# Routing half of the batches beside the first stage, and the other half beside the first expert tiles

## What is computed

```python
emb = word_emb[input_ids] + pos_emb
g_j = relu(mean_g(adj_j @ word_emb[ids_j]) @ W_j.T + b_j)      # three graphs
h = layernorm(concat([emb, broadcast(g_1, g_2, g_3)]) @ W_proj.T + b_proj) * gamma + beta
u = layernorm(h)
h = h + causal_conv(u, k) + u * bias                           # k: 128 taps per channel
x = layernorm(h)
top2, idx = top_k(x @ Wr.T, 2);  w = softmax(top2)
h = h + sum_k w[k] * (gelu(x @ Wi[idx[k]].T + bi) @ Wo[idx[k]].T + bo)
```

## Time and profile before

| | us |
|---|---|
| median of three runs (989.84 to 992.35) | 991.18 |
| span of the profiled execution | 995.9 |
| first stage, to the end of the last projection | 349.5 |
| convolution, to its last matmul | 413.3 |
| routing and first fetch, to the first up matmul | 502.4 |
| 71 tiles, to the last down matmul | 979.5 |
| last scatters | 996.0 |

### The profile page before, as it was taken

How to read it: one execution, slowest core, us unless ns; L and a number is a source line. 1 busy time by engine, 2 the same in 40 slices (tenths; PEclk the granted TensorE clock), 3 DMA queues, 4 the chain that set the end, 5 groups by cost and what they waited for, 6 DMA issues and landing times.

```text
span 995.9 us, 22850 instructions
## 1 busy us (share of the span) xinstructions
PE 869.3 (87%) x7469; PEld 822.9 (83%) x7469; DVE 656.0 (66%) x2142; ACT 536.0 (54%) x1271; POOL 644.7 (65%) x552
## 2 busy tenths in 40 slices
PE   3959898998898739893889999999999999999993
PEld 2959898998898738892679999999999989898993
DVE  3167857776867565978756776666667656666662
ACT  1222223213312325599667777777777767677761
POOL 6777777777777300100067886777778768788886
PEclk9957556556756669996699999999999999999997
DMA  8437547457465429855946446745744543343454
GB/s 245 131 87 248 179 153 257 136 200 225 157 207 195 126 86 282 225 166 131 245 101 149 61 60 158 191 61 122 199 83 63 130 96 61 59 60 59 61 57 44
DMA packets 99788, 138.31 MB, mean 139 GB/s; under 512 B 13427, under 2 KB 81430, under 8 KB 97654
## 3 DMA queue, kind: packets, MB, share of 16 engines
q0 software_dynamic: 39552, 53.26, 28.1%
q1 hardware_dynamic: 59142, 73.59, 24.3%
q10 hardware_dynamic: 1008, 10.34, 2.8%
HBM read 98.14 MB, written 39.02 MB: 138 GB/s over the span
## 4 chain that ended last, share of the span: by engine, by line
PE 29%; DMA 22%; POOL 22%; issue 12%; DVE 8%; ACT 4%; DVEq 2%; SPq 1%; POOLq 0%; ACTq 0%
DMA out<-Hs,id_s 20%; POOL ev_g L521 13%; POOL emb_g L512 5%; PE bank L799 3%; PE bank L801 3%; PE bank L800 3%; POOL blob L537 3%; PE bank L780 2%; PE bank L781 2%; PE bank L784 2%; PE bank L783 2%; PE bank L782 2%; DVE hstats L1157 2%; ACT adj_s L956 1%; PE bank L763 1%
## 5 line engine op out<-in xcount | busy, mean ns | idle before, releaser
L975 ACT ACTIVATE Hs<-bank,U 128x256 bf16<-128x256 f32 x426 | 214.0, 502 | 126.0 <-PE bank L784 126.0
L551 POOL DMA_INDIRECT out<-Hs,id_s x142 | 233.5, 1645 | 65.6 <-issue 45.6
L537 POOL DMA_INDIRECT blob<-xtab_d,id_g x142 | 151.6, 1068 | 122.7 <-DVEq L1340 79.6
L521 POOL DMA_INDIRECT ev_g<-in_word_emb,ids_i x192 | 189.7, 988 | 58.5 <-issue 57.9
L976 ACT ACTIVATE Hs<-bank,U 128x256 f32<-128x256 f32 x426 | 216.4, 508 | 0.0
L799 PE MATMUL bank<-U,Hs 128*128 128x192 bf16 x852 | 210.0, 246 | 0.3 <-issue 0.3
L801 PE MATMUL bank<-U,Hs 128*128 128x192 bf16 x852 | 208.8, 245 | 0.0
L800 PE MATMUL bank<-U,Hs 128*128 128x192 bf16 x852 | 208.5, 245 | 0.0
L1362 DVE TENSOR_TENSOR Hs<-Hs 128x512 bf16<-128x512 f32 x213 | 146.8, 691 | 92.1 <-ACT Hs L976 92.0
L780 PE MATMUL bank<-wst,U 128*128 128x256 bf16 x426 | 116.6, 274 | 1.3 <-DVE wst L1351 1.3
L781 PE MATMUL bank<-wst,U 128*128 128x256 bf16 x426 | 116.7, 274 | 0.0
(11 more groups left out here) (216 smaller groups left out, 1643.2 us busy)
## 6 DMA issues: line engine op xcount, KB each, us to landing
adj_s<-in_adj SPq DMA_DIRECT2D x48, 256.0 KB, 7.3
ev_g<-kpad_d SPq DMA_DIRECT2D x24, 512.0 KB, 5.8
U<-blob_d SPq DMA_DIRECT2D x14, 771.0 KB, 5.0
wst<-in_wsrc SPq DMA_DIRECT2D x8, 1344.0 KB
blob_d<-blob ACTq DMA_DIRECT2D x7, 1443.0 KB
U<-blob_d SPq DMA_DIRECT2D x14, 672.0 KB, 5.7
xtab_d<-U SPq DMA_DIRECT2D x4, 1552.0 KB, 17.0
out<-Hs SPq DMA_DIRECT2D x4, 1536.0 KB, 12.8
```

The source lines that it names most:

```text
L521: pool.indirect_dma_start(ev_g[:, p, j, b, :], None, t["word_emb"], bass.IndirectOffsetOnAxis(ap=ids_i[:, 1 + j, i * Q + b:i * Q + b + 1], ...
L537: pool.indirect_dma_start(xg_f[:, q % RX, h, :], None, xtab_d, bass.IndirectOffsetOnAxis(ap=id_g[:, 2 * q + h:2 * q + h + 1], axis=0)).the ...
L551: pool.indirect_dma_start(out, bass.IndirectOffsetOnAxis(ap=id_s[:, 2 * q + h:2 * q + h + 1], axis=0), yo[:, q % RY, h, :], None, compute_ ...
L975: f(hh[w][:, d, :], ps, ACT.Gelu, bias=bi[:, d:d + 1])
```

## The change

The batches are cut into two halves of 32. The convolution, the scores, the ranks and the sorting are written as a generator `route(x)` for each engine, which does one small step per call, and `advance(route, n)` does n steps.

- `route(0)`, for batches 0 to 31, is interleaved with groups 8 to 15 of the first stage; the tables `beside` say how many steps stand before and behind the group's projection (on ACT: at its end).
- Of the first half's choices, only full tiles are taken, the first `TA = 25` of them; what is left over goes with the second half's. The number of tiles stays 71.
- `route(1)`, for batches 32 to 63, is interleaved with tiles 1 to 24 by `pieces(q)`. Before tile 25 all engines finish it and start the fetches anew.
- A matmul of the convolution still moves 128 columns (now four channels' worth of 32, of which one is wanted), so that each half takes 192 of them.
- `W3` goes from 3 to 2, `RY` (rooms for results) from 4 to 3. The PSUM banks are dealt out anew: the graph results share bank 0 with the column means, so `graph_vectors(i)` waits for the copy of the means of group i + 1; `project` has one pair of banks.
- The splitting of expert weights goes on one expert per group (0 to 7), with two rooms; SP issues all stores of them. The Toeplitz loads of the first half are issued by ACT, those of the second by SP between the weight reloads.
- Loops on registers are written out.

```diff
@@ constants @@
-RING = 4
+RING = 5
-W3 = 3
+TA = 25
+W3 = 2
+WK = 3
-RY = 4
+RY = 3
...
@@ sync @@
+            for q in range(WB, NT):
+                while given < min(UNITS, 4 * q - 1):
+                    next_toep(given)
+                    given += 1
+                if q == 10:
+                    store_rows(1)
+                if q == TA - 1:
+                    store_inputs(1)
+                if q == TA:
+                    sp.wait_ge(eid_done, 2)
+                reload_up(q, q % WB)
+                if q > WB:
+                    reload_down(q - 1, (q - 1) % WB)
...
@@ tensor @@
             def graph_vectors(i, p):
-                pe.wait_ge(cs_ready, i + 1)
+                pe.wait_ge(cs_ready, min(i + 2, NQ))
...
+            def route(x):
+                pe.wait_ge(rows_done, NA * (x + 1))
+                if x:
+                    pe.wait_ge(eid_done, 1)
+                at_conv = conv_bank[x]
+                for u in range(UNITS):
+                    c = u // 2
+                    pe.wait_ge(turned[x], u + 1)
+                    if u % 2 == 0:
+                        after(pe, conv_read[x], c - len(at_conv) + 1)
+                    place = bank[at_conv[c % len(at_conv)]]
+                    for k in range(CC):
+                        at = u % 2 * CC + k
+                        n = min(128 // HALF, 2 * CC - at)
+                        last = mm(place[:, at * HALF:(at + n) * HALF], tp[x][u % 2][:, k, :],
+                                  Ut[x][:, u * CC + k:u * CC + k + n, :].rearrange("p c b -> p (c b)"), start=True, stop=True)
+                    last.then_inc(conv[x], 1)
+                    yield
...
+                pe.wait_ge(conv_read[x], CHUNKS)
+                turn_pair(0)
+                yield
+                for h in range(PAIRS):
+                    if x == 0 and h + 1 < PAIRS:
+                        turn_pair(h + 1)
+                    score(h)
+                    if x == 1 and h + 1 < PAIRS:
+                        turn_pair(h + 1)
+                    yield
...
+                for g in range(TG):
+                    pe.wait_ge(hot_p_ready[x], g + 1)
+                    pe.wait_ge(hot_s_ready[x], g + 1)
...
+            early = route(0)
+            beside = {8: (0, 4), 9: (2, 4), 10: (2, 4), 11: (2, 4), 12: (2, 9), 13: (0, 8), 14: (1, 9), 15: (0, 8)}
...
+                graph_features(i)
...
+                advance(early, beside.get(i, (0, 0))[0])
+                project(i, p)
...
+                advance(early, beside.get(i, (0, 0))[1])
...
+            def pieces(q):
+                if 1 <= q <= 6:
+                    return 2, 0, 2
+                if 7 <= q <= 11:
+                    return 1, 1, 1
+                if q == 12:
+                    return 1, 0, 1
+                if q in (14, 15):
+                    return 1, 0, 0
+                return (1, 0, 1) if 16 <= q < TA - 1 else (0, 0, 0)
...
+                up_tile(q)
+                if q + 1 < NT and q + 1 != TA:
+                    turn_rows(q + 1)
+                advance(late_route, n[0])
+                if q > 0:
+                    down_half(q - 1, 0)
+                    advance(late_route, n[1])
+                    down_half(q - 1, 1)
+                advance(late_route, n[2])
+                if q + 1 == TA:
+                    for _ in late_route:
+                        pass
+                    turn_rows(TA)
@@ scalar @@
+                if x == 0:
+                    act.wait_ge(kpad_stored, 32)
+                    act.wait_ge(w_lo, E - 1)
+                    for u in range(RING):
+                        load_toep(act, x, u)
+                    act.wait_ge(w_out[0], 16 * E // 2)
...
+                for g in range(TG):
+                    scaled(g)
+                    for b in range(2 * g, 2 * g + 2):
+                        row_part(b)
+                    yield
+            beside = {8: 6, 9: 6, 10: 6, 11: 6, 12: 8, 13: 9, 14: 9, 15: 8}
...
@@ vector: the steps of route(x): 12 additions, statistics, variances, choices and sum,
@@ scales, slots, shares, 16 pairs of one-hots, ids @@
+            beside = {8: (0, 2), 9: (1, 2), 10: (1, 2), 11: (1, 2), 12: (1, 2), 13: (0, 2), 14: (1, 9), 15: (0, 8)}
...
+                if 1 <= i <= E:
+                    split_lo(i - 1)
+                if i + 2 < NQ:
+                    row_sums(i + 2, p)
+                advance(early, beside.get(i, (0, 0))[0])
+                rows(i, p)
...
+                advance(early, beside.get(i, (0, 0))[1])
...
+            def pieces(q):
+                if q == 1:
+                    return 0, 1
+                if 2 <= q <= 6:
+                    return 1, 1
+                if q == 7:
+                    return 1, 1
+                if q == 8:
+                    return 1, 0
+                if q == 13:
+                    return 1, 1
+                if q == 14:
+                    return 0, 1
+                if q == 15:
+                    return 1, 1
+                return (1, 1) if 16 <= q < TA - 1 else (0, 0)
...
                 split_hidden(q, q % W3, (0, 2))
-                if 0 < q < NT - 1:
+                advance(late_route, n[0])
+                if 0 < q < NT - 1 and q + 1 != TA:
                     transposed(q + 1, (q + 1) % W3)
                 split_hidden(q, q % W3, (4,)).then_inc(hid, 1)
                 if q > 0:
                     bias_out(q - 1)
+                advance(late_route, n[1])
```

More of the change, by code:

```diff
@@ L86, in after @@
                 eng.wait_ge(semaphore, value)
[L88 to L95, removed]
         out_rows = out[0:B * S, :].rearrange("(b s) d -> b s d", s=S)
@@ L657, in _ @@
-            column_means(0, 0)
-            steps(pe, NQ // 2, pair, last=1)
-            pe.wait_ge(rows_done, NQ)
-            def chunk(it, s):
-                c = it * RING + s
-                pe.wait_ge(turned, c + 1)
-                for k in range(CC):
-                    n = 2 if k < CC - 1 else 1
-                    last = mm(bank[6 + s % 2][:, k * B:(k + n) * B], tp[:, s % 2, k, :],
-                              Ut[:, bass.ds(c * CC + k, n), :].rearrange("p c b -> p (c b)"), start=True, stop=True)
-                last.then_inc(conv, 1)
@@ L696, in score @@
-            def score(i):
-                p = i % 2
-                g = next(k for k, (first, n) in enumerate(GROUPS) if i * Q < first + n)
-                pe.wait_ge(xnT_ready, i + 1)
-                after(pe, chosen, g - 1)
-                for h in range(Q // 2):
-                    at_h = (i * Q - GROUPS[g][0] + 2 * h) * E
-                    for r in range(XR):
-                        last = mm(bank[3 + g % 2][:, at_h:at_h + 128], xnT[:, p, XR * h + r, :], wr[:, r, :], start=r == 0, stop=r == XR - 1)
-                last.then_inc(logits, 1)
@@ L883, in _ @@
-            column_copy(0, 0)
-            steps(act, NQ // 2, pairs, last=1)
-            def turn(it, s):
-                act.wait_ge(toep_in[s], 16 * (it + 1))
-                after(act, conv, it * RING + s - 1)
-                f(tp[:, s % 2, :, :], reverse(toep[:, s, :, :]), ACT.Copy).then_inc(turned, 1)
-            turn(0, 0)
-            turn(0, 1)
-            normal(NQ - 1, 1)
-            for s in range(2, RING):
-                turn(0, s)
-            with act.Fori(1, NCH // RING) as it:
-                for s in range(RING):
-                    turn(it, s)
@@ L948, in _ @@
[L948 to L957 removed]
+                p = e % 2
+                act.wait_ge(w_in[p], 48 * (e // 2 + 1))
@@ new lines, in _ @@
+            early = route(0)
+            beside = {8: 6, 9: 6, 10: 6, 11: 6, 12: 8, 13: 9, 14: 9, 15: 8}
+            column_copy(0, 0)
+            for i in range(NQ):
+                p = i % 2
+                embedding_copy(i, p)
+                if i < NQ - 1:
+                    column_copy(i + 1, 1 - p)
+                graphs(i, p)
+                if i == 0:
+                    filter_decay()
+                    filter_sine(1)
+                if i > 0:
+                    normal(i - 1, 1 - p)
+                if i < E:
+                    split_hi(i)
+                advance(early, beside.get(i, 0))
@@ L959, in row_hi @@
+            normal(NQ - 1, 1)
+            for _ in early:
+                pass
+            f(junk[:, :], mean_w[:, 0:1], ACT.Gelu)
             def row_hi(q):
@@ L1394, in _ @@
                     bias_out(q - 1)
+                advance(late_route, n[1])
+                if q + 1 == TA:
+                    for _ in late_route:
+                        pass
+                    row_lo(TA)
+                    transposed(TA, TA % W3)
             bias_out(NT - 1)
```

1079 lines of the change are left out of this document (544 added, 535 removed).

## The result

| | before | after | forecast |
|---|---|---|---|
| median, us | 991.8 | 1185.3 (1182.2 to 1186.8) | 1074 |
| ratio of the times | 1 | 1.1937 [1.188, 1.1994] | 1.083 |
| span of the profiled execution | 995.9 | 1182.2 | 1078.9 |
| first up matmul, F | 502.4 | 552.2 | 472.4 |
| what the second half adds, X | | 136.5 | 113 |

The change makes the kernel 19% slower. The direction was right, the size was not: 193 us more where 83 were forecast, and the time lies far above the range. By the sum of the prediction, X = 1182.2 - 995.9 - (552.2 - 502.4) = 136.5. So of the 103 us that the forecast's span is short, 80 are in F and 23.5 in X. F didn't fall by 30 us, it rose by 50.

The account below looks back on a forecast made before the run. Gathers were taken to pace the first stage, with TensorE 90% busy, and TensorE the tiles. Span 995.9 us, less 30 for an earlier first up matmul, plus 113 from the second half, times 0.9953: 1074 us, range 1050 to 1095.

Parts of the forecast that it names:

- Groups 0 to 7: First stage: the added wait for the next column means' copy costs 1 us (bounds 0 and 6.4); VectorE's weight split is hidden.
- Groups 8 to 12: First stage beside the first half's convolution: 27.2 us per group in 9 to 12, plus 5 us for late Toeplitz loads.
- Group 14: First stage: one-hots queue behind VectorE's rows, TensorE idles about 17.5 us; group 13's projection to group 15's takes 78 us.
- From group 15 to the tiles: After group 15's projection, in series: rows 13.9, picks 11.4, table store 8, fetch to first up matmul 6.9; 40 us.
- Tiles 1 to 6: Second half's convolution beside these tiles: 24 units of 1.8 us add 43 us to TensorE, plus 2 for waits.
- Tiles 7 to 12: Second half's turn and score: 16 pairs at 1.25 us add 20 us, plus 2 for the wait on the last addition.
- Tiles 13 to 15: VectorE's choices, scales and slot step delay copies that TensorE needs; 2 x 2.1 us caught up, 14 us added.
- Tiles 16 to 23: Two picks per tile give ACT 8.7 us of work against 6.6 per tile, adding 17 us.
- The last tiles: Tile stage: output ring of three instead of four costs 0; additional expert weight reloads cost 4 us (0 to 20).
- the rival with the full clock: Full clock holds in groups 8 to 13, waits by order stay: 1034 us; chance 0.23.
- the one paced by the gathers: Gathers still pace the first stage, TensorE's free time takes the first half's work: 962 us; chance 0.06.
- The rival with late transfers: Toeplitz loads, weight reloads and refill at their upper bounds add 30 us: 1104 us; chance 0.14.

Follow-up runs that it names:

- The load order: Kernel after, with SyncE issuing the load of expert i before the store of expert i-1: 1149.2 us, ratio 1.1555.
- the new bank: Kernel after, with graph results of groups 0 to 7 in PSUM bank 3, so graph_vectors waits only for its own group's column copy: 1144.9 us, ratio 1.1511.
- three repairs: Kernel after, with expert loads ahead of stores, a separate bank for early graph results, and picks ahead of projection in groups 14 and 15: 1110.8 us, ratio 1.1182.
- The picks' repair: Kernel after, with one-hots ahead of rows in groups 14 and 15 and group 15's picks ahead of its projection: 1160.1 us, ratio 1.1664.

## Why the prediction was wrong, and where it was right

- **Groups 0 to 7: the step that failed.** "Bounds 0 and 6.4; I take 1" priced the added wait by the 0.17 us copy and its 0.8 us delay, as if the copy came as early as before. I asked who is queued behind the wait on TensorE, but not what is queued ahead of the copy on ScalarE, and ahead of that on SyncE. The next sentence, that the split is "hidden", went by VectorE's busy share and left out the store and the load around it. The step cost 57 us where 1 was taken. The load order, the new bank and both together (with the picks) gave 36, 40 and 75 us, and group 8 back at 204.9.
- **Groups 8 to 12** lost 13 us more than forecast. The sum per group was close: 27.7, 29.4 and 31.0 us measured, 27.2 forecast; from the end of group 8's projection to that of group 9's it took 38.4 where 32.2 were due. I gave the first five Toeplitz loads 5 us, bounds 0 and 10, as a matter of bandwidth. What the trace shows is that ScalarE stands while it issues them, 9.9 us; moving them gave F 2.8.
- **Group 13**: 27.6 us forecast, 33.9 measured. Two terms were too small. A step of turn and score, 11 records in my count, takes 1.5 us and not 1.25; and at a granted clock of 0.55 from the graph vectors on, the rest of the group took some 21 us for 17.2.
- **Group 14** was right in mechanism and size: 17.5 us idle forecast, 17.0 measured, and from group 13's projection to the one of 15 78 us forecast, 79 measured. That the picks can be had earlier by their order alone was shown too; the ids, left behind `rows(15)`, kept some 12 us of that from F.
- **From group 15 to the tiles**: 44 us for the 40 forecast. Norm, picks and store took 13.5, 11.4 and 7.9 for 13.9, 11.4 and 8. The fetch took 10.6 (541.68 to 552.23) for 6.9, with four weight loads and several Toeplitz loads issued beside it. That the weight loads slow it isn't borne out: with the picks first they are issued 8 to 12 us ahead of the fetch, and it still took 9.6 (523.80 to 533.39). The cause stays open.
- **Tiles 1 to 6**: 45 forecast, 44.1 measured, TensorE full: right. Only the floor of 11 us right below was not seen.
- **Tiles 7 to 12**: 22 forecast, 29.5 measured. It is the same step of turn and score: 16 of 1.5 us (672.71 to 674.22 in tile 9) are 24 for my 20, and TensorE waits 3.6 us for my 2, all at tile 7, where the clock falls as well.
- **Tiles 13 to 15**: 14 forecast, 20.9 measured. The mechanism was right, VectorE's copies queued behind the choices and slots. TensorE's two waits for them are 15.7 us; I had let 2 x 2.1 us be caught up by VectorE's slack. No experiment separates these terms.
- **Tiles 16 to 23**: 17 forecast, 23.4 measured. ScalarE is the pacer, as forecast; the sum of 8.7 us of its work per tile left no gap, and the tile took 9.15.
- **Tile 25**: 11 forecast, 13.1 measured. **The last tiles**: "the same here: 0" for the ring and 4 for the weight reloads. From tile 26 to tile 70 the kernel after takes 10 us more than before, and its tail 5 less. Luck helps here: the sum is close to my 4, but the 10 us vary from trace to trace, and no run parts the ring from the reloads.
- **The rivals.** TensorE's clock in groups 8 to 13 stayed as forecast, partly lost in every group, so the rival with the full clock falls, and so does the one paced by the gathers. The rival with late transfers had the right kind of cause, but not the place.
- **The whole.** With three repairs F is 479 and the time 1111: 37 us above the forecast. Of this 22 are X and 6.6 F. The rest is the factor between span and median, which I took as 0.9953 and which came out above 1: in every run the time is about 1.8 us more than the span of the same execution, while the profiled span of before, 995.9 us, is longer than that kernel's median time. That F comes so close is luck in part. The picks' repair takes off what the groups from 8 on and the fetch had cost too much, some 24 us; with the 57 us gone alone, F would be about 552 - 57 = 495 by these numbers (an estimate, not run). The forecast was right that the design loses, and wrong about its queues.

## What to carry to other kernels

A wait that is added on a short instruction costs what stands ahead of that instruction in its own engine's order, and ahead of the transfers it needs in theirs; follow the chain to the end before pricing it by the instruction's own time. When a chain of steps is moved forward, move its last step too. Before work is cut in two to hide it, ask which of its costs shrink with the size: here half the batches took 150 us where all had taken 158, and hiding that half beside an engine already 90% busy brought the first tile forward by 16 us. In a queue that holds stores which wait and loads which don't, issue the loads first.

## What the runs showed of the hardware

- The time of fp32 matmuls with a new 128 x 128 weight each is the same with 32 columns as with 128: 13.66 and 13.65 us a tile at a granted clock of 1.00.
- Fewer columns can cost time: with 32 for 128 the granted clock of group 10 went from 0.82 to 0.54, and the group from 27.7 to 39.1 us, with TensorE busy 39.4 of 40 us.
- Convolution matmuls of 128 columns between the one-column ones didn't bring the clock back: 16 records took 3.7 us there, as at the lower level.
- A transfer that ScalarE issues itself can hold it for microseconds: two issues took 9.25 us, the three before them 2.9 us.
